# Attention rows split into fp16 halves one batch ahead of their transposes, and layer 0's normed rows stored ahead of the residual

## The reference, cut to what matters

```python
def attention(h):                 # per sequence, T = 165 rows, one head of 256
    x = layernorm(h)
    q, k, v = x @ Wq + bq, x @ Wk + bk, x @ Wv + bv
    q, k = rope(q), rope(k)
    p = softmax(q @ k.T / 16, causal)
    return (p @ v) @ Wf + bf      # added to h
def experts0(h):                  # top group, both experts of it, gated
    x = layernorm(h)
    return sum(gate[e] * swiglu(x, e) for e in chosen(x))   # added to h
```

## Time and profile before

| what | us |
| --- | --- |
| median of 3 runs | 773.11 (772.79 to 773.18) |
| the profiled execution | 775.75 |
| its span, from the first to the last instruction | 773.4 |
| PE busy | 708.4 (92%) |
| first tile of layer 0's experts on PE | from 137.57 |
| first `maxima` of the attention | from 361.62 |
| last `maxima` of the attention | from 459.82 |

### The profile page before, as it was taken

The page is one execution under the profiler, slowest core; times in us unless marked ns, Lnnn a source line. Parts: engine busy times, 40 slices in busy tenths (PEclk is TensorE's granted clock), DMA queues, the critical chain, the costliest instruction groups (busy, mean ns, idle before and its releaser), DMA issues.

```text
span 773.4 us, 18105 instructions
## 1 busy us (share of the span) xinstructions
PE 708.4 (92%) x6013; PEld 620.4 (80%) x6014; DVE 447.8 (58%) x1222; ACT 365.3 (47%) x865; POOL 271.0 (35%) x251
## 2 busy tenths in 40 slices
PE   5989964899999999989899998799999999999981
PEld 5869954789888887667788987788888888888871
DVE  4898786334444344437797777845454545455540
ACT  5899453343333433343667666243434343344430
POOL 2301200222233223214355440225556555564431
PEclk9999997899999999999999999799999999999996
DMA  9996998114122211127841469212233233323235
GB/s 260 232 191 73 129 164 268 45 29 119 28 32 41 36 22 28 21 45 202 170 48 11 53 78 294 68 37 42 42 55 55 41 45 50 55 44 45 36 36 153
DMA packets 42181, 66.20 MB, mean 86 GB/s; under 512 B 3648, under 2 KB 29232, under 8 KB 41584
## 3 DMA queue, kind: packets, MB, share of 16 engines
q0 software_dynamic: 22272, 39.19, 33.6%
q1 hardware_dynamic: 19664, 25.93, 10.7%
q10 hardware_dynamic: 192, 0.38, 0.2%
HBM read 65.80 MB, written 23.35 MB: 115 GB/s over the span
## 4 chain that ended last, share of the span: by engine, by line
PE 76%; DVE 12%; DMA 4%; ACT 4%; issue 2%; POOL 1%; POOLq 0%; SPq 0%; DVEq 0%
PE PS L1148 16%; PE PS L1161 15%; PE PS L855 14%; PE PS L892 8%; PE PS L1507 3%; PE PS L2443 3%; PE PS L870 3%; PE PS L2457 2%; DMA xs<-Y 2%; PE PS L1534 1%; ACT Y L2161 1%; PE PS L1457 1%; PE PS L1133 1%; DMA X<-in_w_dram 1%; PE PS L1515 1%
## 5 line engine op out<-in xcount | busy, mean ns | idle before, releaser
L1161 PE MATMUL PS<-X 128*128 x720 | 125.7, 273 | 1.9 <-ACT X L1230 1.9
L1148 PE MATMUL PS<-X 128*128 128x256 f16 (+1 forms) x768 | 122.7, 265 | 0.9 <-DVE X L1250 0.5
L1319 POOL DMA_INDIRECT sum<-X,dest x45 | 89.1, 1980 | 96.1 <-ACT X L1230 81.0
L1220 ACT ACTIVATE X<-PS,X 128x256 f32<-128x256 f32 (+1 forms) x192 | 72.8, 463 | 103.3 <-PE PS L1148 103.3
L855 PE MATMUL PS<-Y,X 128*128 128x256 f16 x960 | 109.0, 274 | 0.0
L855 PEld LDWEIGHTS PS<-Y,X 128*128 x960 | 94.4, 98 | 11.2
L1148 PE MATMUL PS<-X,Y 128*128 128x256 f16 (+1 forms) x384 | 100.2, 264 | 0.0
L1161 PE MATMUL PS<-Y,X 128*128 x360 | 98.2, 273 | 0.0
L1148 PEld LDWEIGHTS PS<-X 128*128 x768 | 71.6, 97 | 11.0 <-issue 1.6
L1161 PEld LDWEIGHTS PS<-X 128*128 128x128 f16 x720 | 70.4, 98 | 10.6 <-issue 2.6
L1119 POOL DMA_INDIRECT sum<-Y,dest x24 | 38.7, 1614 | 111.5 <-DVE Y L1052 107.9
(11 more groups left out here) (401 smaller groups left out, 1339.5 us busy)
## 6 DMA issues: line engine op xcount, KB each, us to landing
X<-in_w_dram POOLq DMA_DIRECT2D x16, 1024.0 KB, 13.7
sum<-h SPq DMA_DIRECT2D x2, 2048.0 KB, 17.0
Y<-in_w_dram POOLq DMA_DIRECT2D x4, 1024.0 KB, 11.6
xs<-Y SPq DMA_DIRECT2D x2, 1040.0 KB, 6.9
xs<-Y SPq DMA_DIRECT2D x2, 1032.0 KB, 12.5
h<-in_txt_dram SPq DMA_DIRECT2D x2, 1024.0 KB, 17.5
Y<-in_patches_dram SPq DMA_DIRECT2D x3, 672.0 KB, 8.4
sum<-h SPq DMA_DIRECT2D x2, 768.0 KB, 15.7
```

The source lines that it names most:

```text
L1148: ins = nc.tensor.matmul(PS[:, 2 * s + c // 2, (c % 2) * T1:(c % 2) * T1 + tokens], part[:, off:off + P], x_[:, slot, k, 0:tokens], start= ...
L1161: ins = nc.tensor.matmul(PS[:, 4 + a, 0:D], h_[:, s, c, a * P:(a + 1) * P], part[:, off:off + D], start=(s == 0 and c == 0 and n == 0), st ...
L1220: ins = nc.scalar.activation(hh1[:, s, c, 0:tokens], PS[:, 2 * s + c // 2, (c % 2) * T1:(c % 2) * T1 + tokens], ACT.Gelu, bias=bias1[:, sl ...
L1319: nc.gpsimd.indirect_dma_start(out=sum1, out_offset=bass.IndirectOffsetOnAxis(ap=dest[:, i:i + 1], axis=0), in_=y1buf[:, u % 2, i - first_ ...
```

## The change

1. Everything that multiplies the normed rows of the attention by a weight is done in fp16 with both factors split into a high half and the rest: `x = xh + xl`, `w = wh + wl`, and `xh*wh + xl*wh + xh*wl` is summed in PSUM. So `project` has 24 fp16 products for 8 in float32, and each `*_values` has 6 for 2. The transposes become four in fp16 for two in float32, and ACT's copies carry 512 fp16 elements for 256 in float32.
2. The split of a text tile is POOL's (`split_text`: a cast and a subtraction, 128x256 each), that of an image tile is DVE's (two operations behind the norm), that of Wq and Wk is one copy on ACT and one subtraction on DVE of 128x1024, that of Wv is POOL's (`split_values`, 128x528).
3. Text tiles are normed one batch earlier (`norm(b + 3)` for `norm(b + 2)`), since `split_text` sits between the norm and the transposes. DVE's `moments_back` moves from batch 1 to 0 and from 5 to 4, and the `stats_of` of late tiles from batches 2 to 4 to 1 to 3.
4. ACT's negations of layer 1's weights begin in batch 2 for batch 0 (`NEGATED1`), and POOL's adding transfers are issued in batches 6, 9 and 12 (`ADD_IN`) for 4, 8 and 12.
5. In layer 0, SP stores the normed rows first, and the residual `h` after the first two gathers have landed (`x_in[0]`).
6. Groups 2 and 3, and 4 and 5, of layer 0's weight casts share a semaphore: each waits for both.

```diff
+NEGATED1 = (0, 0, 1, 1, 1, 1, 1, 2, 1, 1, 2, 1, 1, 2, 1, 0)
+ADD_IN = (6, 9, 12)
...
+        def w0_rounded(g):
+
+            return (w0_cast[g], 16) if g < 2 else (w0_cast[1 + g // 2], 32)
...
         def sp_rest(sp):
-            for t, n in ((0, BATCH), (BATCH, IT)):
-                sp.wait_ge(h_added, t + n)
-                sp.dma_start(sum0[t * P:(t + n) * P].rearrange("(t p) n -> p t n", p=P), h[:, t:t + n, :])\
-                    .then_inc(sum_based, 16)
             sp.wait_ge(pay_ready, 1)
             for t, n in ((0, 8), (8, 8), (BATCH, IT)):
                 sp.wait_ge(pay_normed, t + n)
                 sp.dma_start(xs0[t * P:(t + n) * P].rearrange("(t p) n -> p t n", p=P), pay[:, t:t + n, :])\
                     .then_inc(rows_stored, 16)
+            sp.wait_ge(x_in[0], 32)
+            for t, n in ((0, BATCH), (BATCH, IT)):
+                sp.wait_ge(h_added, t + n)
+                sp.dma_start(sum0[t * P:(t + n) * P].rearrange("(t p) n -> p t n", p=P), h[:, t:t + n, :])\
+                    .then_inc(sum_based, 16)
...
-                for bank, w_, done in ((0, wq, q_psum), (1, wk, k_psum)):
+                for bank, w_, done in ((0, wq2, q_psum), (1, wk2, k_psum)):
                     for m in range(KC):
                         for k in range(KC):
-                            ins = nc.tensor.matmul(PS[:, bank, m * SEQ:(m + 1) * SEQ], w_[:, k, m * P:(m + 1) * P],
-                                                   xTb[:, slot, k, :], start=(k == 0), stop=(k == KC - 1))
+                            for n, (wh, xq) in enumerate(((0, k), (0, KC + k), (1, k))):
+                                ins = nc.tensor.matmul(PS[:, bank, m * SEQ:(m + 1) * SEQ], w_[:, wh, k, m * P:(m + 1) * P],
+                                                       xTb[:, slot, xq, :], start=(k == 0 and n == 0),
+                                                       stop=(k == KC - 1 and n == 2))
...
             def norm(b, asked):
 
                 act.wait_ge(scales_ready, 6 + asked)
-                act.wait_ge(xn_tr, NF + b + 1)
+                wait_from(act, xn_split, b - 1)
                 normal(xnF[:, b % 2, :], h[:, b, :], b, P).then_inc(xn_ready, 1)
...
+            def split_text(b):
+
+                pool.wait_ge(xn_ready, NF + b + 1)
+                if b >= 2:
+                    pool.wait_ge(xn_tr, AHEAD + b - 1)
+                nc.gpsimd.tensor_copy(xn2[:, b % 2, 0, :], xnF[:, b % 2, :]).then_inc(own_rounded, 1)
+                pool.wait_ge(own_rounded, b + 1 + (b > 0))
+                nc.gpsimd.tensor_tensor(xn2[:, b % 2, 1, :], xnF[:, b % 2, :], xn2[:, b % 2, 0, :], ALU.subtract)\
+                    .then_inc(xn_split, 1)
...
             def norm_image(n):
                 t = BATCH + n
-                nc.vector.tensor_scalar(xnF[:, 2 + n, :], h[:, t, :], mv[:, t, 0:1], rstd[:, t:t + 1],
-                                        ALU.subtract, ALU.mult).then_inc(xi_ready, 1)
+                chain.link(nc.vector.tensor_scalar(xnF[:, 2 + n, :], h[:, t, :], mv[:, t, 0:1], rstd[:, t:t + 1],
+                                                   ALU.subtract, ALU.mult))
+                chain.link(nc.vector.tensor_copy(xi2[:, n % 2, 0, :], xnF[:, 2 + n, :]))
+                nc.vector.tensor_tensor(xi2[:, n % 2, 1, :], xnF[:, 2 + n, :], xi2[:, n % 2, 0, :], ALU.subtract)\
+                    .then_inc(xi_ready, 1)
...
+                if b == 0:
+                    moments_back(4, MIDDLE[0] - 3, MIDDLE, 6 + len(MIDDLE))
                 if b == 1:
-                    moments_back(4, MIDDLE[0] - 3, MIDDLE, 6 + len(MIDDLE))
                     norm_image(2)
-                if 2 <= b < 5:
-                    stats_of(LATE[b - 2::3])
+                if 1 <= b < 4:
+                    stats_of(LATE[b - 1::3])
+                if b == 4:
+                    moments_back(8, NT - 8, LATE, NT)
                 if b == 5:
-                    moments_back(8, NT - 8, LATE, NT)
                     norm_image(3)
```

More of the change, by code:

```diff
@@ L327, in build @@
         xnF = rx.take([IT + 2, D])
-        xTi = rx.take([KC, IT, P])
-        xTb = rx.take([2, KC, SEQ])
+        xTi = rx.take([2 * KC, IT, P], F16)
+        xTb = rx.take([2, 2 * KC, SEQ], F16)
         qkT = rx.take([2, 2, KC, SEQ])
@@ L343, in build @@
         rsum = rx.take([2, 2])
+        xn2, xi2 = rx.take([2, 2, D], F16), rx.take([2, 2, D], F16)
+        wqk2 = stage[:, 1, :].bitcast(F16).rearrange("p (h n) -> p h n", h=2)
+        wq2, wk2 = (wqk2[:, :, i * KC * D:(i + 1) * KC * D].rearrange("p h (k n) -> p h k n", k=KC) for i in range(2))
+        wvx2 = wqk.bitcast(F16)[:, 0:2 * KC * PAYV].rearrange("p (h k n) -> p h k n", h=2, k=KC)
+        ident2 = stage[:, 0, CW - P // 2:CW].bitcast(F16)
+        turned2 = PS[:, 7, :].bitcast(F16)
         rg = Region(X, XE)
@@ L396, in build @@
         d_moved = sem("d_moved")
-        w0_cast = [sem(f"w0_cast{i}") for i in range(W0C // CAST)]
+        w0_cast = [sem(f"w0_cast{i}") for i in range(4)]
         dve_negated = sem("dve_negated")
@@ L1514, in text_values @@
                 for k in range(KC):
-                    ins = nc.tensor.matmul(PS[:, 2, 0:PAYV], xTb[:, slot, k, IMG:SEQ], wvx[:, k, :],
-                                           start=(k == 0), stop=(k == KC - 1))
+                    for n, (xq, wh) in enumerate(((k, 0), (k, 1), (KC + k, 0))):
+                        ins = nc.tensor.matmul(PS[:, 2, 0:PAYV], xTb[:, slot, xq, IMG:SEQ], wvx2[:, wh, k, :],
+                                               start=(k == 0 and n == 0), stop=(k == KC - 1 and n == 2))
                 ins.then_inc(v_psum, 1)
@@ L1525, in image_values @@
                 for k in range(KC):
-                    ins = nc.tensor.matmul(PS[:, 5, 0:PAYV], xTi[:, k, n, :], wvx[:, k, :], start=(k == 0), stop=(k == KC - 1))
+                    for j, (xq, wh) in enumerate(((k, 0), (k, 1), (KC + k, 0))):
+                        ins = nc.tensor.matmul(PS[:, 5, 0:PAYV], xTi[:, xq, n, :], wvx2[:, wh, k, :],
+                                               start=(k == 0 and j == 0), stop=(k == KC - 1 and j == 2))
                 ins.then_inc(vi_psum, 1)
@@ L1691, in negate @@
             def negate(b):
-                for n in range(b + 1 if b else 0, min(b + 2, W1W // CW)):
+                for n in range(sum(NEGATED1[0:b]), sum(NEGATED1[0:b + 1])):
                     act.wait_ge(*w1_landed(n * CW // W1N))
@@ L1721, in act_attention @@
             norm(1, 2)
+            norm(2, 2)
             image(1)
@@ L1728, in run @@
                 exps(b)
[L1729 to L1730 removed]
+                if b < BATCH - 3:
+                    norm(b + 3, 2 if b < 1 else 3 if b < 5 else 4)
                 normalise_p(b, slot)
@@ L1798, in pool_attention @@
                     image_bias(IMAGE_BIAS.index(b))
-                if b and b % (W1N // CW) == 0:
-                    add(b * CW // W1N - 1)
+                if b in ADD_IN:
+                    add(ADD_IN.index(b))
             add(E1 - 1)
```

65 lines of the change are left out of this document (44 added, 21 removed).

## The result

| | runs | median, us | lowest to highest |
|---|---|---|---|
| before, beside it | 5 | 773.18 | 772.79 to 775.27 |
| changed kernel | 5 | 769.45 | 765.92 to 769.73 |

The ratio is 0.9918, with a 95% interval of 0.9889 to 0.9948: faster by 0.5 to 1.1%, about 6 us (4.0 to 8.6). The forecast of 760.3 us had the sign and twice the size (three times, by the two medians), and its range (755.5 to 767.5) does not hold the median. The profiled execution took 766.62 us, its span is 764.8 us where before's was 773.4.

The account below looks back on a forecast made before the run. PE, busy 92% of the span, was taken to wait at the hand-over's store and in the attention's PE-DVE-POOL ring. Terms -6.3 - 1.2 + 1.1 - 8.0 + 1.3 + 0.3 = -12.8 us gave 760.3 us, range 755.5 to 767.5.

Parts of the forecast that it names:

- Rows ahead of the residual: Hand-over to layer 0's experts: rows' store lands sooner, -6.3 us, and PE's clock no longer drops, -1.2 us.
- rivals A and D: Hand-over: A, the store does not gain, 767.8 us, chance 0.1; D, residual late, 0 to 3 us, no separate chance.
- PE, DVE and the ring in late batches: Attention batches 7 to 14: cheaper projections take 0.30 us off the PE-DVE-POOL ring; 5.6 us each, 44.8 in all.
- rival C: Attention: POOL takes over the ring through a slow cast and subtraction; slower, 777 us at s = 4; chance 0.04.
- PE leaves the path: Attention batches: PE falls from 5.6 to about 4.8 us in a plain batch; the ring or DVE sets the pace.
- Preparation of the attention: Before the first maxima: two image tiles' casts and subtractions on DVE delay them by 1.1 us (0.5 to 2.5).
- 0 each: Attention's preparation: ACT's copy and DVE's subtraction for Wq and Wk fit in idle time, costing 0 each.
- DVE in a batch: Attention: DVE's work puts batches 0 to 6 at 45.4 us; with late batches 90.2 for 98.2, -8.0.
- Held by POOL: Attention: POOL's added work holds DVE's root operations once more, 0.65 us, at worst five times.
- PE's clock: Attention batches 0, 4 and 6: longer PE pauses lower its clock, +1.3 us (0 to 4).
- The -8.0 as one sum: Attention, all 15 batches: 90.2 us for 98.2, counting together the end of ACT's batch 0 block and cheaper products.
- Rival B: Attention does not gain: held DVE roots and clock-halving pauses cost 5 us more than put, 765.3 us; chance 0.15.

Follow-up runs that it names:

- after_again: The changed kernel run once more without a further edit, for a second trace and more times; 767.84 us, 0.9904 of before.
- rows_first_only: The kernel before with only the order of SP's stores changed, normed rows ahead of the residual; 766.77 us, 0.9920 of before.
- high_times_high: The changed kernel with only the high-by-high products in the query and key projections, 8 per batch for 24; 765.80 us, 0.9891 of before.
- weights_split_in_idle: The changed kernel with VectorE's subtraction for Wq and Wk moved behind the second of ScalarE's preparation copies; 764.68 us, 0.9864 of before.
- values_low_half_zero: The changed kernel without GpSimd's subtraction for the value weights' low half, which ScalarE fills with zeros; 763.25 us, 0.9865 of before.
- text_low_half_zero: The changed kernel without GpSimd's subtraction for the text rows' low half, which is left zero; 764.45 us, 0.9888 of before.
- weights_split_later: The changed kernel with a wait meant to delay the Wq and Wk subtraction, already satisfied, so nothing moved; 768.09 us, 0.9926 of before.
- residual_first_again: The changed kernel with the old order of the stores, keeping the split attention and moved negations; 774.31 us, 0.9991 of before.
- rows_and_negations: The kernel before with the normed rows stored first and the negations moved, attention unsplit; 762.94 us, 0.9849 of before.

## Why the prediction was right or wrong

*Rows ahead of the residual: right.* Forecast -6.3 and -1.2. In A and B the changed kernel gains 8.2 us (7.3 and 0.9), after_again 6.5, rows_first_only 6.9; the ratio of rows_first_only is worth 6.2 (4.2 to 8.2). The gather starts at 126.14, not behind 129, and nothing waits for the residual: rivals A and D fall.

*PE, DVE and the ring in late batches: right in size, nearly so in kind.* 5.65 us for 5.6, E 45.07 for 44.8, spacing 72 ns. GpSimd did not take the ring: its cast takes 0.40 and its subtraction 0.67, and rival C falls. "PE leaves the path" is true but for 0.15 us: VectorE still waits that long for the projections, and high_times_high, which takes the wait away, gains 0.2 us in a plain late batch.

*Preparation of the attention, +1.1: wrong, it was +3.3 to +3.7.* The two image tiles cost what the step said. The term that failed is "0 each": the subtraction for Wq and Wk does lie in VectorE's idle time, but not outside GpSimd's. It lengthened the last send, and the cover that I had looked at was that of one engine alone (0.8 to 1.2 us, weights_split_in_idle). And `split_values` was taken to be ready ahead of its use, which it is; that it holds a root while it runs was not asked (0.9 to 1.4 us, values_low_half_zero).

*DVE in a batch, and Held by POOL: wrong.* Batches 0 to 6 were put at 45.4 us and took 50.0 in the profiled execution, 47.8 where the clock held. "One more such meeting, 0.65, and at worst five" became a loss of 1.74 us from the text's subtraction alone (text_low_half_zero), with the bias addition's meetings besides: the excess of roots and image norms is 3.6 us where before had 0.8, so 2.9 more and not 0.65, near the "at worst five", though not all of it need lie on the path. The Trainium skill, "SBUF — State Buffer", section "Who interferes with whom", states that a VectorE instruction with two inputs in the SBUF contends with a GpSimd instruction that reads it, and that the one issued first holds the other for its whole length. The rows agree: the operation of 348.57 began behind GpSimd's subtraction and ended with it, and GpSimd's cast of 352.00 began 0.02 us behind a subtraction of VectorE and took 0.67 us for 0.40. By the same section an instruction with at most one SBUF input, outside the modes that use two ports, does not contend; the statistics, 1.40 us either way, agree.

*PE's clock, +1.3: about right.* Against weights_split_in_idle, where it cost next to nothing, D is longer by 2.3 us in the profiled execution (0.7 in batch 0, 1.3 in batch 5, 0.3 in batch 6), by 1.6 in after_again and by 1.3 in weights_split_later. In residual_first_again batch 2 alone lost 1.8.

*The -8.0 as one sum: the step that hid the error.* It took the end of ScalarE's stall in batch 0 and the cheaper products together. Apart, the stall is worth 1.9 us by its ratio (0.9 to 2.9) and 2.85 in the trace, and the halves give 3.8 in the late batches and take 3.3 to 3.7 in preparation and 2.9 to 3.5 in the early ones (D 49.4 to 50.0 for 46.5). Stage by stage the split, with the earlier norms and roots that go with it, thus costs 2.4 to 3.4 us, of which the lower clock is 1.6 to 2.3. By the ratios of after_again and rows_and_negations, 0.9904 for 0.9849, it is 4.3 us, give or take 1.9. In weights_split_in_idle the stages come out level with those of rows_and_negations (+2.5, +1.3 and -3.8 us in C, D and E), as the two ratios do. Rival B, attention without gain, is what happened, by operations that were held and a lower clock as it said, and by the late send, which it did not name: its 765.3 is still 2.5 to 4 us under the medians of the changed kernel's three sets (767.84 to 769.45).

*Two readings and the noise.* The forecast took the two long early batches of before for 8 to 9 us and batch 10 for the shortest. Between maxima, batch 1 took 11.25 us and batch 5 7.98, and batches 4 and 7 took 5.36 and 5.39. It also took runs to agree within 0.05%, from three of them; the five beside the changed kernel spread over 0.3%, the changed kernel's over 0.5%.

*What stays open.* In the profiled executions the changed kernel is ahead of before by 9.1 us (766.62 for 775.75), by the three ratios 5.7 to 7.4. The stages up to A, the same in all kernels, spread over 4 us from one execution to the next; what moves them was not tried.

## What to carry to other kernels

A change of several parts is to be forecast part by part against a baseline that has the other parts: here reordering the stores and the negations gives 1.5%, and the halves, the largest edit, take part of it away as they stand, and pay nothing that can be told even when mended. An operation that VectorE does in its idle time is free only when GpSimd is not then doing something that it holds up and that others wait for: the subtraction of 1.22 us cost 0.8 to 1.2 in its first place and nothing that shows 2.4 us later. Once TensorE has all but left the path, cheaper products pay little (0.2 us a batch for 1.15 us of work), while the operations that prepare them stand on the engines that are now waited for.

## What the runs showed of the hardware

- A VectorE subtraction of 128x1024 with both inputs in the SBUF, started 0.05 us ahead of GpSimd's issue of an indirect transfer, made the issue take 2.60 us for 1.55; in weights_split_in_idle, apart, it took 1.55. All eight traces in which the two stand side by side show 2.60. The Trainium skill, "SBUF — State Buffer", section "Who interferes with whom", has it that a probe showed no stall of transfers by such an operation, and infers as the reason that it takes the read interface only, where the making of descriptors needs the write interface; here the measurement decides against it.
- GpSimd's subtraction of 128x528 held a VectorE operation of 0.18 us, begun 0.20 us behind it, for 1.04 us, to within 0.04 us of the subtraction's end.
- The same pause of TensorE, 2.23 and 2.24 us, was followed by 1.2 GHz in one execution (granted clock 0.50 from 394.80 to 398.20, so 0.63 over 394 to 397 us) and by 2.4 GHz in another (1.00). Lines of changed and weights_split_in_idle, busy time of the engines, then PEclk:

```profile
394.00:397.00 3.00, 2.18 (x10) 1.70 (x11) 2.93 (x11) 1.79 (x7) 2.37 (x4) 0.63 0.00 0
```

```profile
394.00:397.00 3.00, 2.56 (x23) 2.38 (x24) 2.90 (x10) 2.49 (x11) 2.52 (x5) 1.00 0.00 0
```
